# Three of sixteen source columns of every sixth edge group come from TensorE in two attention passes

## The reference

```python
h = (x @ W).reshape(-1, heads, out_ch)
alpha_s = (h * a_s[None]).sum(-1)
alpha_d = (h * a_d[None]).sum(-1)
e = alpha_s[src] + alpha_d[dst]
e = jnp.where(e > 0, e, NEG_SLOPE * e)
m = jax.ops.segment_max(e, dst, num_segments=num_nodes)
w = jnp.exp(e - m[dst])
denom = jax.ops.segment_sum(w, dst, num_segments=num_nodes)
alpha = w / (denom[dst] + 1e-16)
out = jax.ops.segment_sum(alpha[:, :, None] * h[src], dst, num_segments=num_nodes)
```

## Time and profile before

| | us |
|---|---|
| median of 3 runs | 13218.92 (13215.43 to 13219.89) |
| profiled execution, its own time | 13244.6 |
| its span | 13242.9 |
| GpSimd busy | 9825.8 (74%) |
| VectorE busy | 6799.1 (51%) |
| ScalarE busy | 4056.7 (31%) |
| TensorE busy | 520.3 (4%) |
| GpSimd indirect DMAs, all passes | 10,350 |

### The profile page before, as it was taken

One profiled execution on the slowest core, in us unless ns is written; L12 is line 12 of the kernel. 1 busy time (PEld: TensorE's weight loads), 2 busy tenths in 40 slices (PEclk: granted clock), 3 DMA queues, 4 the chain that ended last, 5 costly groups with the idle time before them and its releaser, 6 DMA issues. The chain is left out here.

```text
span 13242.9 us, 103860 instructions
## 1 busy us (share of the span) xinstructions
PE 520.3 (4%) x1768; PEld 340.0 (3%) x1768; DVE 6799.1 (51%) x10545; ACT 4056.7 (31%) x3972; POOL 9825.8 (74%) x10362
## 2 busy tenths in 40 slices
PE   3000001100000300000010000000000000000001
PEld 1000000100000200000000000000000000000000
DVE  2777876377777533333333333343333336656656
ACT  4333333233333311111112111111111113666663
POOL 7777776777777677777777777777777776777775
PEclk9999999555555655555555555555555555555555
DMA  8445444344444222222212222222222223444443
GB/s 333 120 123 128 123 123 107 90 123 123 123 123 123 63 66 65 63 65 66 62 45 61 63 61 61 59 49 58 62 62 62 63 62 88 161 160 156 160 160 115
DMA packets 976807, 1317.32 MB, mean 99 GB/s; under 512 B 660843, under 2 KB 676674, under 8 KB 962815
## 3 DMA queue, kind: packets, MB, share of 16 engines
q10 hardware_dynamic: 557731, 803.76, 18.7%
q0 software_dynamic: 334400, 373.85, 14.8%
q1 hardware_dynamic: 83996, 134.02, 2.8%
HBM read 651.23 MB, written 659.53 MB: 99 GB/s over the span
## 5 line engine op out<-in xcount | busy, mean ns | idle before, releaser
L1851 POOL DMA_INDIRECT c_y<-g_tab,srcs x4545 | 4301.9, 947 | 1388.2 <-issue 1388.2
L2305 POOL DMA_INDIRECT c_y<-h_tab,srcs x1547 | 1463.9, 946 | 506.6 <-issue 471.7
L815 POOL DMA_INDIRECT c_y<-h_tab,srcs x1531 | 1448.2, 946 | 467.3 <-issue 467.3
L815 POOL DMA_INDIRECT first_y<-h_tab,srcs x1452 | 1373.5, 946 | 445.4 <-issue 442.9
L1883 DVE TENSOR_TENSOR c_s<-c_y,c_ad 128x64 f32<-128x64 f32 (+1 forms) x297 | 79.3, 267 | 1881.4 <-DMA c_y<-g_tab,srcs 1850.7
L1966 ACT ACTIVATE c_ex<-c_de 128x64 f32<-128x64 f32 (+1 forms) x297 | 67.4, 227 | 3171.8 <-issue 2852.7
L1919 DVE COPY c_w_in<-c_ex 128x64 f32<-128x64 f32 (+1 forms) x297 | 66.4, 224 | 1609.0 <-ACT c_ex L1966 1609.0
L1927 DVE TENSOR_TENSOR_SCAN c_acc<-c_r,c_w_in 128x1156 f32<-128x1156 f32 (+1 forms) x297 | 753.0, 2535 | 14.6
L837 DVE TENSOR_TENSOR_SCAN c_q_all<-c_mask,c_q_in 128x408 f32<-128x408 f32 (+2 forms) x792 | 733.7, 994 | 16.6 <-issue 9.1
L881 DVE TENSOR_TENSOR_SCAN c_acc<-c_r,c_w_in 128x408 f32<-128x408 f32 (+2 forms) x792 | 731.0, 986 | 8.2
L928 ACT ACTIVATE c_q_in<-c_q_raw 128x1552 f32<-128x1552 f32 (+1 forms) x198 | 596.6, 3013 | 280.9 <-DVE c_q_in L897 198.6
(11 more groups left out here) (405 smaller groups left out, 6429.7 us busy)
## 6 DMA issues: line engine op xcount, KB each, us to landing
rows_d<-c_row ACTq DMA_DIRECT2D x97, 2048.0 KB
c_y<-g_tab SPq DMA_DIRECT2D x12288, 0.3 KB
rows_d<-c_row ACTq DMA_DIRECT2D x291, 576.0 KB
rows_d<-c_row ACTq DMA_DIRECT2D x194, 784.0 KB
c_q_raw<-q_start ACTq DMA_DIRECT2D x194, 776.0 KB, 6.2
c_y<-h_tab SPq DMA_DIRECT2D x6144, 0.2 KB
c_y<-g_tab ACTq DMA_DIRECT2D x6144, 0.3 KB
q_start<-first_y SPq DMA_DIRECT2D x97, 776.0 KB, 8.8
```

Source lines behind the costliest of these rows:

```text
L815: nc.gpsimd.indirect_dma_start(y[:, g % NY, k, 0:D], None, h_tab, source(g, k))\
L1851: nc.gpsimd.indirect_dma_start(y[:, g % NY, k, :], None, g_tab, source(g, k))\
L2305: nc.gpsimd.indirect_dma_start(y[:, g % NY, k, :], None, h_tab, source(g, k))\
```

## The change

In c4 and c5 GpSimd no longer fetches three of the 16 columns of slot 5 (k = 11, 12, 13), except in round 0. TensorE makes them. The 384 source numbers of these columns are broadcast to all partitions (`wanted`, a DMA from a new table `srcs_d`, which `begin` makes with three more column reads and three stores). For each of the 98 nodes c of a partition VectorE compares `wanted` with the node's number (`node`) and so writes a 128 × 384 matrix of zeros and ones (`hot`); TensorE multiplies the 98 slices of `gt` with these and adds them up in PSUM, [72, 384]. VectorE copies this to SBUF, TensorE turns it in three transposes, and VectorE copies the result into `y`.

The 98 comparisons come in 14 *halves* of seven, with two buffers: half h may be made when TensorE has used half h − 2. They stand in VectorE's order after the groups j = 1 to 5 of a round: three halves after each of j = 1 to 4, two after j = 5. The two copies stand after j = 0 and j = 1 of the next round. `hot`, `wanted` and the copy lie in `ad_raw`, which is free by then. The last round makes no halves. ScalarE loads `wanted` for the next round after group 5, when the last half is made.

```diff
@@ begin: SyncE, VectorE
+                    for k in range(NPE):
+                        sp.dma_start(pe_src_i[k * NACT:(k + 1) * NACT, :],
+                                     by_column[PE_SLOT * GW + PE_K + k:NY * GW * NACT:NY * GW, :]).then_inc(src_loaded.h, 16)
...
+                for k in range(NPE):
+                    sp.dma_start(srcs_d[:, k * P:(k + 1) * P], pe_src[k * NACT:(k + 1) * NACT, :]).then_inc(places_stored.h, 16)
@@ gat_edges
-        taken = SYNC_SLOTS + [ACT_SLOT]
+        by_pe = bd is None
+        taken = SYNC_SLOTS + [ACT_SLOT] + [PE_SLOT] * (NPE * by_pe)
...
+            spare = ad_raw[:].rearrange("p t h -> p (t h)")
+            hot = spare[:, 0:14 * PE_W].rearrange("p (b r n) -> p b r n", b=2, r=7)
+            cols_t, wanted = spare[0:TG, 14 * PE_W:15 * PE_W], spare[:, 15 * PE_W:16 * PE_W]
@@ GpSimd
-                    for k in range(by_pool(g, taken)):
+                    for k in range(by_pool(g, taken) + (NPE if by_pe and g == PE_SLOT else 0)):
@@ TensorE
+                def columns_of(n):
+                    for half in range(NHALF):
+                        pe.wait_ge(*made(n, half))
+                        pe.nop(nofuse=True)
+                        for c in range(half * 7, half * 7 + 7):
+                            last = nc.tensor.matmul(pa[0:TG, 0:PE_W], gt[:, c, :], hot[:, half % 2, c % 7, :],
+                                                    start=c == 0, stop=c == NC - 1)
+                        last.then_inc(hot_used.h, 1)
...
+                if by_pe:
+                    columns_of(0)
+                    with pe.Fori(1, NACT - 1) as n:
+                        turn_columns(n)
+                        columns_of(n)
+                    turn_columns(NACT - 1)
@@ VectorE
-                with v.Fori(0, NGRP // NY) as n:
+                def six_steps(n, first=False, last=False):
                     for j in range(NY):
                         step(piece(n * (NY // 2) + j // 2, j % 2), j, n)
+                        if by_pe and j == 0 and not first:
+                            v.wait_ge(*used(n - 1, NHALF - 1))
+                            v.tensor_copy(cols_t, pa[0:TG, 0:PE_W]).then_inc(hot_made.h, 1)
+                        if by_pe and j == 1 and not first:
+                            v.wait_ge(*hot_used(n * 15))
+                            v.tensor_copy(y[:, PE_SLOT, PE_K:PE_K + NPE, :].rearrange("p k f -> p (k f)"), pb[:, 0:NPE * TG])\
+                                .then_inc(hot_made.h, 1)
+                        if by_pe and j and not last:
+                            one_hot(n, range(3 * j - 3, min(3 * j, NHALF)), first)
+
+                def one_hot(n, parts, first):
+                    for half in parts:
+                        if half == 0:
+                            v.wait_ge(*wanted_loaded(n * 16 + 16))
+                        if half >= 2:
+                            v.wait_ge(*used(n, half - 2))
+                        elif not first:
+                            v.wait_ge(*used(n - 1, NHALF - 2 + half))
+                        for c in range(half * 7, half * 7 + 7):
+                            end = v.tensor_scalar(hot[:, half % 2, c % 7, :], wanted, node[:, c:c + 1], None, ALU.is_equal)
+                        end.then_inc(hot_made.h, 1)
@@ ScalarE
+                    elif j > NPART and target and by_pe:
+                        act.wait_ge(*made(n, NHALF - 1))
+                        load_wanted(n + 1)
```

More of the change, by code:

```diff
@@ L671, in _ @@
                 v.tensor_scalar(places[:, 1, :], src_f[:], 4.0 * TG, None, ALU.mult).then_inc(vs.h, 1)
+                v.wait_ge(*vs.before("pe_src"))
+                v.tensor_copy(pe_src[:], pe_src_i[:]).then_inc(vs.h, 1)
             @block.tensor
@@ L1793, in block_diagonal, with gat_edges @@
         st.close()
-    def gat_edges(tag, rows, bd=None):
+    def gat_edges(tag, rows, gt, bd=None):
         H, J1 = HG, JG + 1
@@ L1866, in _, with turn_columns @@
                                              stop=True).then_inc(e_scored[b].h, 1)
+                def columns_of(n):
[6 more added lines that the diff above has]
+                        last.then_inc(hot_used.h, 1)
+                def turn_columns(n):
+                    pe.wait_ge(*hot_made(n * 16 - 1))
+                    pe.nop(nofuse=True)
+                    for k in range(NPE):
+                        last = nc.tensor.transpose(pb[:, k * TG:(k + 1) * TG], cols_t[:, k * P:(k + 1) * P], ident[0:TG, 0:TG])
+                    last.then_inc(hot_used.h, 1)
+                if by_pe:
+                    columns_of(0)
[3 more added lines that the diff above has]
+                    turn_columns(NACT - 1)
                 fix_on_tensor(pe)
@@ L1949, in _ @@
                 v.wait_ge(*ready(3))
-                with v.Fori(0, NGRP // NY) as n:
+                def six_steps(n, first=False, last=False):
                     for j in range(NY):
                         step(piece(n * (NY // 2) + j // 2, j % 2), j, n)
+                        if by_pe and j == 0 and not first:
[18 more added lines that the diff above has]
+                        end.then_inc(hot_made.h, 1)
+                six_steps(0, first=True)
+                with v.Fori(1, NACT - 1) as n:
+                    six_steps(n)
+                six_steps(NACT - 1, last=True)
                 for pc in LASTS:
@@ L1993, in load_places, with load_wanted, group @@
                     act.dma_start(at, places_d[bass.ds(n + NTABLE + NSYNC, 1), :]).then_inc(at_read.h, 16)
-                def group(n, j, more=True):
+                def load_wanted(n):
+                    act.dma_start(wanted, srcs_d[bass.ds(n + 1, 1), :].to_broadcast([P, PE_W])).then_inc(wanted_loaded.h, 16)
+                def group(n, j, more=True, target=True):
                     i, b = n * (NY // 2) + j // 2, j % 2
@@ L2019, in _ @@
                 for j in range(NY):
-                    group(NACT - 1, j, False)
+                    group(NACT - 2, j, target=False)
+                for j in range(NY):
+                    group(NACT - 1, j, False, False)
                 for pc in LASTS:
```

43 lines of the change are left out of this document (31 added, 12 removed).

## The result

The changed kernel takes 13398.4 us (median of 4 runs, 13394.5 to 13400.05), the kernel before 13219.0 in the same comparison (13215.4 to 13219.9): +179.4 us, ratio 1.0136, 95% interval 1.012 to 1.0152. The forecast was 13375. The profiled execution of after took 13394.5 us (span 13392.8), that of before 13244.6: +150 only. The gap of 30 us between the two differences is mostly (25.6 us) the distance of before's profiled execution from its median, and that is an offset between executions. In stages that the change leaves alone a column of GpSimd takes 944 ns in one execution and 946 or 947 in another, for its whole length; over 10,350 columns that is about 25 us.

A forecast was written before the change was run, and what follows sets the result against it. GpSimd's column fetches bound c4 and c5, the ScalarE–VectorE chain 9.6 us a round behind. The chain becomes the bound: +146 for both passes, +9 first stage, +155, said as 13375 us; range 13245 to 13620.

The forecast's parts named there:

- The comparisons: On VectorE in c4 and c5: comparisons of 384 elements start 0.30 us apart, 2.1 us for a half.
- The products: On TensorE in c4 and c5: the first half of each burst takes 7.0 us, the others 4.5.
- The cover: After j = 1, 2, 3 the halves lie beside ScalarE's DMAs, where 14.8 us are free, and cost nothing.
- The round: ScalarE and VectorE in turn, c4 and c5: 106.5 − 0.64 + 11.6 + 4.2 = 121.7 us, over GpSimd's 112.7.
- The pass's end: Groups 90 to 97 of a pass, with all rows there, take 115.0 us instead of 125.7: −11.
- GpSimd beside the comparisons: GpSimd waits 0.15 us twice a column, some 20 columns a round: 6 us, making 118.7, hidden by the chain's 121.7.
- The first stage: New single-element loads before the zeros cost 13.5 us, of which 4.6 are hidden: +9, between 0 and 36.
- the held port: Rival, 10%: what GpSimd needs is held through a half; its mean in c4 1,200 ns, time outside 13245 to 13620.
- the wait for a whole comparison each time: Rival, 12%: GpSimd waits 0.3 us twice for 20 columns a round, 124.7 us a round: +265, 13485.
- The clock that stays down: Rival, 5%: TensorE's clock stays low because it stands before each burst; time outside 13245 to 13620.
- Fits into the slack: Rival, 5%: comparisons after j = 4 and 5 take at most 6.8 us, GpSimd sets the pace: −113 + 9, 13115.
- no change: Rival, 5%: the time stays the same, if the comparisons after j = 4 and 5 take between 10 and 12 us.

The follow-up runs named there:

- one product of seven: The changed kernel with only the first of each half's seven products made, all comparisons, waits and copies kept: 13268.9 us, +24.8 to the kernel before.
- The first spread: The changed kernel with its fourteen halves made after j = 0 to 3 as 4, 4, 3, 3, none after j = 4 and 5: 13282.7 us.
- both copies first: The 4, 4, 3, 3 placing of halves after j = 0 to 3, with the copy into `y` also after j = 0, ahead of the halves: 13187.6 us.

## Why the prediction was right

- **The bound of before** was read rightly: taking the columns away alone gave −110 (predicted 113 less 9 for the first stage, 3.6 measured). The break-even of 10.9 us for the comparisons after j = 4 and 5 had left the first stage's 9 out; with them it is 10.6.
- **The comparisons.** 0.30 us apart and 2.1 a half were taken; they start 0.329 apart and take 0.42, 2.39 a half. I had read a slope of 0.5 ns an element from two other shapes.
- **The products.** In c4 and c5 of after the 2,940 products have 5,880 records, two each, as I had taken. TensorE's first half of a burst holds VectorE's third half up until 6.7 to 7.0 us after its first product (medians after j = 1 to 4). My 7.0 for that half and the 18 of a burst were estimates that no run shows; the 4.5 of each further half agrees with other products, twelve records in 4.49 us at 1.00. In after a burst's first half, which begins at 0.50, takes 6.5 us (median; 4.5 to 7.6), the second 4.51 at 1.00, and a burst of three 15.8 (15.1 to 16.7). The stretch after j = 4 is 11.9 us (median; 11.1 to 12.7), 11.6 predicted; the two halves after j = 5 4.7, 4.2 predicted. That this wait makes a good part of the loss is shown by the kernel with one product of seven: 4.6 of the 10.3 us after j = 4.
- **The cover** after j = 1, 2, 3 held: 22.1 to 22.5 us there, as before.
- **The round** was 122.9 and 122.4, 121.7 predicted. After j = 4 it is 18.8 and 19.2 (19.5 predicted), after j = 5 14.9 and 13.7 (13.1 predicted). The second term is the mis-sized one. I took 8.9 us for the whole floor there (its rows give 5.25 + 3.5 = 8.75). ScalarE's loop ends in the same place: its DMA is out at 7.9 us, the branch takes 3 to 4, in c4 a table load with 1.4 follows, so it can't be at the exponential before 12 to 13 us. In c4 of before, where I looked, the branch was 0.2 us, and c5, where it was 3.6 and hidden, I didn't read. In the changed kernel the load of the wanted columns stands ahead of the branch and waits for the last comparison, so that branch and table load come on top; taking it away gave −38.6 us, 33 of them in the passes. That 13.1 came so near is in part luck: the 8.9 us of the earlier trace rows hold c4's table load, which I didn't know of. VectorE alone is ready earlier, as the last two rounds of each pass show, which ScalarE has outside its loop, with no branch and no table load: 11.7 to 12.2 us.
- **The pass's end**: −14.3 and −14.6, −11 predicted, since eight groups outside the loop need 111.4 and not 115.0 us.
- **GpSimd beside the comparisons**: its mean is 966 ns, 1,000 to 1,050 predicted. A column beside a train takes 1.02 instead of 0.944. So the excess is 0.04 us for each of the two times that I let it wait; I had taken 0.15. The 1.29 us in the earlier trace rows are a column that stood to the end of one operation; a column held through fourteen, 5.02 us, goes beyond that. Which of the two outcomes a train has, let in or held, no run settles in general. The first spread lies 120 us above the version that has both copies first and holds no train (+64.0 against −56.5). So my 10% was given to something that exists, but with the order of the changed kernel it comes in 1 of 150 trains; and where it came there in 27 of 30, with the copies one group later, the chain hid it.
- **The first stage.** The new loads take 6.7 us for three, and the load before them 15.1:

```profile
11.42 15.10 SPq L451 DMA_DIRECT2D begin_src_i<-in_src  x1
26.57 6.74 SPq L454 DMA_DIRECT2D begin_pe_src_i<-in_src  x3
33.35 26.69 SPq L459 DMA_DIRECT2D q_start<-first_y  x13
...
267.38 0.99 POOL L527 DMA_INDIRECT q_start<-begin_q_rows,start_i  x1 [5.23 <-issue]
```

  The zeros begin at 33.35 instead of 25.08, and the first scatter comes at 267.4 (273 predicted) instead of 263.8. The way was right (8.3 us less the 4.6 hidden is 3.7), the 13.5 us for the loads too much.
- **The sum** was +155, measured +179. Of the 24 us, 21 are in the passes (167 against 146), −5 in the first stage, and 9 outside the sum, of which the offset described at the start gives 7.6.
- **The rivals**: the held port and the wait for a whole comparison each time are out as the cause of this time: GpSimd needs 113.9 us a round, and with all columns fetched the time stays the same though GpSimd has more to do. The clock that stays down is out by the windows, which go from 0.50 to 1.00 within a burst. "Fits into the slack" and "no change" are out by the time itself.

## What to carry to other kernels

Work that is moved to an idle engine costs what it pushes, so ask where in the round the engine idles and who waits behind it: ninety-eight comparisons cost +179 us in one order and −57 in another, with the same instructions. A queue's idle time says little on its slack if another engine's loop end, with its branch and its table load, is hidden in the same place. And look at the longest single instruction beside the mean: 1004 instead of 966 ns was one column of 5 us in the 90 of nearly every round.

## What the runs showed of the hardware

- VectorE's fourteen comparisons of 128 x 384 hold a column of GpSimd to their end or nearly so (it lasts 4.3 to 5.6 us instead of 0.95) in 27 of the 28 trains that follow directly on a copy of 72 x 384 from PSUM, in each of four kernels, and in 0 to 2 of 30 elsewhere; with a small copy between in 4 of 28, with a wait and a copy of 128 x 216 in none. Nearly all held columns end 0.12 us after the last comparison, where they start up to 0.29 us after the copy does, or 0.82, where they start 0.33 us after it or later. The trains of 21 comparisons in the kernel with one product of seven, none of which follows on that copy, hold none. Whether the 72 partitions, the source in PSUM or the lack of a gap does it is open; I didn't try them apart. The copy of 128 x 216 comes from PSUM as well and stands directly ahead of a train in after, where 1 of 28 holds.
- The instruction behind the branch at ScalarE's loop end comes after 0.2 us in c3 of before and after and in c4 of before, after 3.6 to 3.9 in c5 of before, 2.9 to 4.1 in c4 and c5 of after and up to 5.3 in the version with both copies first. Each slow one has a packet of 8,192 bytes on the instruction queue in the gap. In before c4 and c5 run the same loop of the program: why the branch is free in one and dear in the other is open. An exponential behind it in c4 has a table load of 1.28 us, in c5 none.
- GpSimd's column takes 944 ns in all of one execution and 946 to 947 in all of another, which is 25 us of this kernel.
- TensorE's granted clock was at 0.50 in the first 3.2 us after a pause of some 6 us, and at 1.00 in the ten after that (after, from 7588.8 us on). Fourteen records of 384 columns took 4.51 us at 1.00.
